# Feed-forward tiles moved into the attention slots of a fused attention and feed-forward kernel

## The reference

```python
q_big = einsum('bshk,hkq->bshq', (layernorm(x) @ Wq.T).reshape(b, s, 16, 128), w_kc_q)
kv_rope = kv_c * cos + rotate_half(kv_c) * sin
scores = einsum('bhsr,bhlr->bhsl', einsum('bshq,hqr->bhsr', q_big, W_qr), einsum('bld,hdr->bhlr', kv_rope, W_kr))
ctx_c = einsum('bhsl,bld->bhsd', softmax(scores), kv_rope)
x = x + einsum('bhsd,hkd->bshk', ctx_c, w_kc_kv).reshape(b, s, 2048) @ Wo.T

def bitlinear158(x, w):               # x: rms norm, rounded to 127 steps of its row maximum; w: -1, 0, 1 times a scale
    return einsum('bsd,od->bso', quant8(rmsnorm(x)), ternary(w))
h = gelu(bitlinear158(layernorm(x), w1))          # 256 -> 1024
x = x + bitlinear158(h, w2)                       # 1024 -> 256
```

## Time and profile before

| | us |
|---|---|
| median of 3 runs | 517.16 (516.45 to 519.42) |
| the profiled execution | 517.95 |
| its span, first to last instruction | 516.2 |
| first block and slots 0 to 7 | 0 to 148.1 |
| slots 8 to 31 | 148.1 to 351.4 |
| last slots, pipeline running empty | 351.4 to 382.5 |
| feed-forward stage | 382.5 to 516.2 |

### The profile page before, as it was taken

One profiled execution on the slowest core, in us unless ns is written; L12 is line 12 of the kernel. 1 busy time (PEld: TensorE's weight loads), 2 busy tenths in 40 slices (PEclk: granted clock), 3 DMA queues, 4 the chain that ended last, 5 costly groups with the idle time before them and its releaser, 6 DMA issues. The chain is left out here.

```text
span 516.2 us, 8571 instructions
## 1 busy us (share of the span) xinstructions
PE 411.6 (80%) x2819; PEld 297.8 (58%) x2819; DVE 354.0 (69%) x833; ACT 224.5 (43%) x393; POOL 272.7 (53%) x234
## 2 busy tenths in 40 slices
PE   3997776799899999999999999987445664655555
PEld 1486654487687868777787878764431232333223
DVE  0627144878877667677676777766437998999994
ACT  0122252245344453535454545433226565765650
POOL 0301502427446374645555564425456999999871
...
DMA packets 62795, 48.93 MB, mean 95 GB/s; under 512 B 51168, under 2 KB 56288, under 8 KB 61728
## 3 DMA queue, kind: packets, MB, share of 16 engines
...
## 5 line engine op out<-in xcount | busy, mean ns | idle before, releaser
L426 POOL TENSOR_TENSOR cl<-cr,ch 128x512 fp32r<-128x512 f32 x64 | 81.1, 1290 | 142.5 <-ACT ch L478 142.5
L846 PE MATMUL hps<-w1q,xqt 128*128 128x512 bf16 x128 | 41.3, 457 | 50.0 <-DMA xqt<-xq 50.0
L587 PE MATMUL hps<-bh,ch 128*128 128x256 f32 x256 | 76.0, 297 | 5.6 <-POOL cl L426 5.6
L542 PE MATMUL ps<-xh,ah 128*128 128x256 f32 x256 | 75.6, 296 | 1.7 <-DVE xl L644 1.4
L588 PE MATMUL hps<-bl,ch 128*128 128x256 f32 x256 | 73.2, 286 | 0.0
L589 PE MATMUL hps<-bh,cl 128*128 128x256 f32 x256 | 73.1, 286 | 0.0
L543 PE MATMUL ps<-xl,ah 128*128 128x256 f32 x256 | 72.0, 281 | 0.0
L544 PE MATMUL ps<-xh,al 128*128 128x256 f32 x256 | 71.9, 281 | 0.0
L465 ACT ACTIVATE qf<-ps 128x512 f32<-128x512 f32 x64 | 38.3, 598 | 71.5 <-PE ps L544 71.3
L478 ACT ACTIVATE ch<-cr 128x512 fp32r<-128x512 f32 x64 | 39.3, 632 | 64.6 <-DVE cr L682 64.6
L542 PEld LDWEIGHTS ps<-xh,ah 128*128 128x128 f32 x256 | 48.9, 191 | 28.5 <-issue 24.0
...
## 6 DMA issues: line engine op xcount, KB each, us to landing
rb<-rinv_d SPq DMA_DIRECT2D x64, 256.0 KB, 3.8
...
rinv_d<-ri SPq DMA_DIRECT2D x128, 2.0 KB, 1.4
...
```

What stands on the lines that cost most here:

```text
L426: pool.tensor_tensor(cl[:, u % 2, :, b * S:(b + 1) * S], cr[:, u % 2, :, b * S:(b + 1) * S], ch[:, u % 2, :, b * S:(b + 1) * S].bitcast(F3 ...
L542: pe.matmul(o, ah[:, c, cols], xh[:, k % 2, c, :], start=(c == 0), stop=False)
L587: pe.matmul(O[:, 0:D], c_h, bh[:, hp, :], start=(hp == 0), stop=False)
L846: m = pe.matmul(hps[j % 2][:, k * 512:(k + 1) * 512], xqt[:, j % 2, c, :], w1q[:, c, k * 512:(k + 1) * 512], start=(c == 0), stop=(c == KC ...
```

## The change

The third block is gone; its work stands in the slots, which now run from 0 to 43 (`LAST`). A tile's feed-forward starts seven slots behind its scores and ends eleven or twelve behind. Per slot n:

- GpSimd: `g_round(n - 9)` (two multiply-adds on 1,024 columns), in even slots `x_round` of tiles n - 6 and n - 5 (each two on 256 columns), the input norm as two multiply-adds, the low parts, `centre(n - 3)`. All subtractions of a mean have become additions of a negative mean.
- TensorE: in odd slots `up` for tile n - 7 (both halves) ahead of contexts and the first half of tile n - 6 at the slot's end; its second half comes after the scores of the next slot. `down(n - 10)` stands behind contexts. In odd slots the second query group now stands ahead of the shifts. `up` shares the two query banks (`USES` lists who takes them in turn), `down` writes the other half of the bank of `project`.
- ScalarE: per pair of slots four gelus of 512 columns in a row, across the end of the odd slot; a square of a gelu tile in every slot, before the exponentials in odd slots; the square of the centred tile n - 4 now ahead of the exponentials.
- VectorE: in odd slots two scale steps and `norms`, 15 steps on up to four columns (two tiles' x and two tiles' gelu) at the slot's end; in even slots two gelu maxima, one ahead of the quadrant sums and one behind, and two scale steps; `finish(n - 11)` at the slot's start. Statistics of the second half of x: two tiles in each of slots 1 to 8, deviations in slot 9.
- SP: two x transposes (odd slots), a gelu transpose and a store ahead of the shift rows.
- kv: eight tiles are turned in the first block, the rest in slots 2, 6, 10, ... in groups of four (`kv_t`, `kvt_out`); `kvt` keeps eight. `cr`, `rb`, `tq` and `qt` have fewer buffers.

The core of the diff:

```diff
@@ bank turns
+        USES = [("x", 0), ("q", 0, 0), ("q", 0, 1), ("x", 1), ("q", 0, 2), ("q", 0, 3)]
+        for n in range(LAST):
+            k, b = n // 2 + 1, 2 * (n % 2)
+            if n % 2 == 0 and tile(n - 7):
+                USES.append(("h", n - 7, 1))
+            if k < NB:
+                USES.append(("q", k, b))
+            if n % 2 and k + 1 < NB:
+                USES.append(("x", k + 1))
+            if k < NB:
+                USES.append(("q", k, b + 1))
+            if turns(n):
+                USES.append(("k", (n + 2) // 4))
+            if n % 2 and tile(n - 7):
+                USES += [("h", n - 7, 0), ("h", n - 7, 1), ("h", n - 6, 0)]
@@ SP
+                    if n % 2 and tile(n - 7):
+                        turn_x(n - 7)
+                        turn_x(n - 6)
+                    if tile(n - 10):
+                        turn_g(n - 10)
+                    if tile(n - 12):
+                        store(n - 12)
...
@@ GpSimd
-                    pool.tensor_scalar(xn[:, t % 2, :], xs[:, t, :], mv[:, t:t + 1, 0], rstd[:, t:t + 1], ALU.subtract, ALU.mult).then_inc(sem["x_normed"], 1)
+                    pool.tensor_scalar(xc[:, :], xs[:, t, :], 1.0, nmean[:, t:t + 1], ALU.mult, ALU.add).then_inc(sem["x_normed"], 1)
+                    pool.wait_ge(sem["x_normed"], 2 * t + 1)
+                    pool.tensor_scalar(xn[:, t % 2, :], xc[:, :], rstd[:, t:t + 1], 0.0, ALU.mult, ALU.add).then_inc(sem["x_normed"], 1)
...
+                def x_round(t):
+                    pool.wait_ge(sem["x_scale_steps"], 2 * (t // 2 + 1))
...
+                    pool.tensor_scalar(xa[:, :], yc[:, t % YR, :], c1[:, t:t + 1], MAGIC, ALU.mult, ALU.add).then_inc(sem["x_scaled"], 1)
+                    pool.wait_ge(sem["x_scaled"], t + 1)
...
+                    pool.tensor_scalar(xq[:, t % 2, :], xa[:, :], 1.0, -MAGIC, ALU.mult, ALU.add).then_inc(sem["x_rounded"], 1)
@@ ScalarE
+                def gelu(t, half):
+                    act.wait_ge(sem["hidden"], 2 * t + half + 1)
+                    if half == 0:
+                        act.wait_ge(sem["norm_steps"], NORM_STEPS * (t // 2 + 1))
...
+                    act.activation(g[:, t % GB, 512 * half:512 * half + 512], turn_bank("h", t, half), ACT.Gelu, scale=hscale(scl, t)).then_inc(sem["gelu_done"], 1)
@@ TensorE
                 def project(u):
                     pe.wait_ge(sem["ctx_lo"], 2 * u + 2)
+                    at_least(pe, sem["outputs"], u - 7)
...
+                def down(t):
+                    pe.wait_ge(sem[f"gqt_turned{t % 2}"], 16 * (t // 2 + 1))
+                    pe.wait_ge(sem["residuals"], min(t + 8, NT))
+                    at_least(pe, sem["outputs"], t)
+                    for c in range(FC):
+                        m = pe.matmul(O[:, D:2 * D], qt[:, t % 2, c, :], w2q[:, c, :], start=(c == 0), stop=(c == FC - 1))
+                    m.then_inc(sem["products"], 1)
@@ VectorE
+                def norms(j):
+                    c = slice(2 if j >= NB else 0, 2 if j < 2 else 4)
+                    v, r, t, m, s = fw[0][:, c], fw[1][:, c], fw[2][:, c], amax[:, j, c], scl[:, j, c]
...
+                    dve.tensor_tensor(v, stat[:, j, c], least[:, c], ALU.max).then_inc(done, 1)
+                    dve.wait_ge(done, n + 1)
+                    rsqrt(dve, v, r, t, done, n + 1)
+                    dve.tensor_tensor(t, r, m, ALU.mult).then_inc(done, 1)
...
+                    if n % 2 == 0 and tile(n - 8):
+                        g_max(n - 7)
+                        g_scale((n - 8) // 2)
+                    if tile(n - 4):
+                        x_max(n - 4)
+                    if n % 2 and tile(n - 5):
+                        x_scale((n - 5) // 2)
+                    if n % 2 and 0 <= (n - 5) // 2 < NB + 2:
+                        norms((n - 5) // 2)
```

657 lines of the change are left out of this document (306 added, 351 removed).

## The result

The changed kernel takes 541.39 us (median of four runs, 538.98 to 544.2) against 517.61 us before: a ratio of 1.046, 95% interval 1.038 to 1.053. I had forecast 513 us and a gain. The profiled execution took 544.2 us for a span of 542.4.

A forecast was written before the change was run, and what follows sets the result against it. TensorE set the old loop; VectorE's longer chain would set the new one. Head 154.6 + slots 8 to 31 300.3 + tail 57 = 511.9 us span; with 1.75 for execution, 513.7, predicted as 513; range 485 to 545 us.

The forecast's parts named there:

- What bounds the kernel now: Slots 8 to 31: TensorE sets the slot at 8.84 us, VectorE has little slack and gets a longer chain every second slot.
- Part 1, the head: Up to turned (TensorE's transpose of the quadrant maxima) of slot 8: 150.6 - 4.4 - 2.6 + 10 + 1 = 154.6 us.
- The 4.4 us off the first block: Head saving: 2.9 us between the query weight halves, 0.7 for other kv turns, 0.8 for the first two input norms.
- Part 2, the even slot: Even slots: exponentials start at 5.4 us behind a 1.28 us table load, then VectorE's chain; 11.05 us in all.
- Part 3, the odd slot: Odd slots: exponentials start at 6.35, VectorE's chain with fifteen norm steps gives 13.85, GpSimd holds 1.2; 15.05 us.
- Does anything else bind?: Loop: TensorE's 22.2 of 26.1 us a pair and its new waits cost nothing, covered by 4 us a pair.
- Part 4, the tail: Behind turned of slot 31: 44.7 us to the last gelu scale, holds, roundings, transpose, down, finish and store; 57 us.
- Plus 1 for holds: Tail, VectorE's chain behind turned of slot 31: 1 us added for GpSimd holding small VectorE steps.
- A: Slower rival: GpSimd holds the odd slots' norms 3.2 us instead of 1.2; 536 us, chance 22%.
- B: Slower rival: a table load lets ScalarE run empty and costs twice its row, 12 x 1.28 more; 528 us, 8%.
- C: Faster rival: no holds and squares fit into waits, 495 us; 467 if VectorE did not bind at all; chance 20%.
- D: Slower rival: TensorE's clock falls in gaps; 26.7 us a pair at 0.83, 44 and 700 in all at worst; 6% with other slower cases.

The follow-up runs named there:

- tail_banks: Changed kernel with the second feed-forward product, from tile 22 on, sent in turn to the two banks that held the scores; median 535.5 us.

## Why the prediction was wrong, by its own steps

**What bounds the kernel now:** right. TensorE set the loop, VectorE had little slack, and its chain became the bound when 15 norm steps were put behind the sums. The sum of the loop, 1.5 us off, is right in part by luck: the usual even slot is 0.4 us shorter than forecast, some 4.7 us in twelve, and the low clock put about 5 us back, 2.4 in slot 9 (its project took 5.1 us for 2.9; the deviations themselves took 2.6 for the 2.8 forecast) and 1.3 and 1.5 in slots 13 and 21.

**Part 1, the head, failed by 11.6 us.** The norms of slots 5 and 7 are exact: both slots take 13.8 us, 8.8 + 5 forecast. The 4.4 us off the first block were nearly right where the clock was the same (tail_banks: 3.4). What failed is a term that the sum didn't have: the clock. 5.4 us are the late rise in the first block, which one execution of the same code did not have. Some 3 are slot 2, at 0.50 behind a wait (2.6 came back when it was filled). The rest lies in slot 6, 11.54 us in place of 8.7, where TensorE idled 4.3 us for the norms of slot 5 before its turned; the project there took 5.3 us and not 2.85.

**Part 2, the even slot:** 10.66 for 11.05. The exponentials started 5.24 us after turned (5.4). The load's full 1.28 us on the path was right in size, but at most 0.84 of it comes back in the even slot itself.

**Part 3, the odd slot:** 15.13 for 15.05, in part by errors that cancel. The exponentials started 6.9 us after turned and not at 6.35 (TensorE waits 1.13 us for GpSimd's input norms, and with it come late the queries and their copy, which stands ahead of the exponentials), and the holds were 0.8 and not 1.2 us. The short scalings took 0.48 and 0.40 us, as the line through the earlier trace rows said.

**"Does anything else bind?" is the step that failed most.** It costed the new waits at nothing because a pair has 4 us of cover, and the cover is the loop's. Behind slot 31 there is none. For the finish of the tile eight back, a wait which the prediction named and put at nothing, TensorE stands idle 10 us there ahead of three projects, and other banks gave back 7.4 us.

**Part 4, the tail, 57 us forecast, 74.4 measured.** To the first gelu scale of the tail's pairs 40.4 us for 29.9 (that wait, above all: 34.3 with other banks, where one of the three is left; and two of the three projects ran at the low clock in part or throughout, 4.5 and 5.4 us for 2.9); two pairs of 10.2 and 9.4 for 8.0 and 6.8 (holds: 8.1 and 7.0 without them); from the last gelu scale to the end 14.4 for 11. In this last piece two products and two finishes stand one behind the other in one half bank, the first held up by a finish that waits for the last norms, and each product takes 1.86 and not 1.04 us, at the low clock. "Plus 1 for holds" was the wrong term: I had priced them in the odd slot, where short scalings meet the norms, and in the tail two full roundings, 2.2 us each, do. The earlier trace rows had shown just that row.

**The rivals.** A had the mechanism, GpSimd holding the norms, and the wrong place: not in the loop, but in the tail's chains. B falls: the load costs its 1.28 us once, by this row and the 22 others that stand between busy work.

```profile
306.07 0.19 ACT L564 ACTIVATION_READ_ACCUMULATOR sqj<-yc 128x1 f32 x1
306.27 1.28 ACT L553 ACT_TABLE_LOAD   x1
307.57 1.09 ACT L553 ACTIVATE pe<-hps 128x512 f32<-128x512 f32 x2
```

It begins 0.01 us after busy work ends, and the next work begins 0.02 us behind it. The Trainium skill, page "ScalarE: Activation LUTs", section "What ACT_TABLE_LOAD costs", adds a drain of 1380 ns; no load of this trace shows one. C had 0.8 us of holds a pair to lose in the loop, and VectorE did bind. D, the clock, was given a few points in a hundred, and it took part in the misses of the head and of the tail, and in the loop. Its worst case was summed too low: 44 us a pair would be 18 us more in each of 11.5 pairs, about 720 us in all and not 700.

The sum of the failures: 17.4 us more in the tail alone turn 513 us into 530, slower, without the clock's share in the head. The gain that I forecast (4 us) was smaller than what I had left unpriced behind the loop.
